# Attention with 32 array rows per head, in units of two heads, on one core

## The reference

```
qkv = layernorm(t) @ w_qkv + b_qkv
attn = softmax((q @ k.T) * HD ** -0.5)
t = t + (attn @ v) @ w_proj + b_proj
```

## Time and profile before

| | |
|---|---|
| median of 3 runs | 281.2 us (280.62 to 281.5) |
| the profiled execution | 279.14 us |
| its span, first to last instruction | 277.3 us |
| mean granted TensorE clock | 0.965 of 2.4 GHz |
| busy | PE 249.7 us (90%), DVE 185.9 (67%), ACT 117.8 (42%), POOL 112.7 (41%) |
| spectral part | 0 to 29.5 us, first tokens and their norm to 36 us |
| attention | 36 to 144 us, first scores at 56.6 us |
| routing, loop, end | 147 to 175, 175 to 258, 258 to 277.3 us |

### The profile page before, as it was taken

How to read it: one execution, slowest core, us unless ns; L and a number is a source line. 1 busy time by engine, 2 the same in 40 slices (tenths; PEclk the granted TensorE clock), 3 DMA queues, 4 the chain that set the end, 5 groups by cost and what they waited for, 6 DMA issues and landing times.

```text
span 277.3 us, 5843 instructions
## 1 busy us (share of the span) xinstructions
PE 249.7 (90%) x2023; PEld 188.2 (68%) x2023; DVE 185.9 (67%) x367; ACT 117.8 (42%) x218; POOL 112.7 (41%) x85
## 2 busy tenths in 40 slices
PE   3999876889999999969888869999999999999982
PEld 3989674777797797658678658455556555554871
DVE  0358699887997998873674883665666666566264
ACT  0370253244153345315523303655765576566303
POOL 8700078672085069100131043265655565653100
PEclk9999995999999999979999798999999999999998
DMA  7989993000000000172388401111111111111163
GB/s 177 248 201 284 273 345 114 0 0 4 2 0 2 0 2 0 53 218 74 111 281 262 143 2 28 28 47 57 43 57 43 53 46 57 42 45 41 40 207 115
DMA packets 24542, 25.97 MB, mean 94 GB/s; under 512 B 5767, under 2 KB 23208, under 8 KB 24520
## 3 DMA queue, kind: packets, MB, share of 16 engines
q1 hardware_dynamic: 20296, 20.30, 24.6%
q0 software_dynamic: 2400, 4.92, 6.0%
q10 hardware_dynamic: 1824, 0.47, 0.7%
HBM read 22.14 MB, written 3.54 MB: 93 GB/s over the span
## 4 chain that ended last, share of the span: by engine, by line
PE 69%; DVE 23%; ACT 2%; issue 2%; DMA 1%; POOL 1%; DVEq 0%
PE bank L1331 10%; PE bank L1359 8%; PE bank L1338 6%; PE bank L1069 5%; PE bank L1222 4%; PE bank L1070 4%; PE bank L1071 4%; DVE main L769 4%; PE bank L1122 4%; PE bank L997 4%; DVE main L758 3%; PE bank L1347 3%; PE bank L1177 3%; DVE main L730 3%; PE bank L1162 2%; PE bank L1045 2%
## 5 line engine op out<-in xcount | busy, mean ns | idle before, releaser
L286 POOL TENSOR_TENSOR rounded<-rounded,cf 128x1536 fp32r<-128x1536 f32 x12 | 38.7, 3243 | 31.0 <-ACT rounded L556 28.3
L1069 PE MATMUL bank<-rounded 128*128 128x256 f32 (+1 forms) x144 | 42.6, 296 | 4.4 <-DVE rounded L764 3.0
L604 ACT ACTIVATE main<-bank 128x512 f32<-128x512 f32 x48 | 28.7, 598 | 37.9 <-PE bank L1071 36.1
L936 DVE COPY main<-main 128x1152 f32 x43 | 33.1, 781 | 16.6 <-issue 14.8
L632 ACT ACTIVATE main<-down_all 128x576 f32 x44 | 30.0, 684 | 28.8 <-PE bank L1359 27.6
L1070 PE MATMUL bank<-rounded 128*128 128x256 f32 (+1 forms) x144 | 41.2, 286 | 0.0
L1071 PE MATMUL bank<-rounded 128*128 128x256 f32 (+1 forms) x144 | 41.1, 286 | 0.0
L758 DVE TENSOR_REDUCE main<-bank 128x2 f32<-128x512 f32 x48 | 31.0, 685 | 7.1 <-PE bank L1122 7.1
L467 POOL DMA_INDIRECT main<-xhat_rows,main x22 | 27.6, 1254 | 19.6 <-PE bank L1319 15.8
L1069 PEld LDWEIGHTS bank<-rounded 128*128 128x128 f32 x144 | 28.2, 196 | 7.7 <-DVE rounded L764 3.5
L475 POOL DMA_INDIRECT pair_rows<-main x20 | 21.7, 1083 | 26.0 <-DVE main L926 26.0
(11 more groups left out here) (164 smaller groups left out, 386.7 us busy)
## 6 DMA issues: line engine op xcount, KB each, us to landing
down_all<-wd SPq DMA_DIRECT2D x16, 288.0 KB, 4.8
main<-wg SPq DMA_DIRECT2D x16, 192.0 KB, 3.2
main<-wu SPq DMA_DIRECT2D x16, 192.0 KB, 2.9
main<-wg SPq DMA_DIRECT2D x16, 96.0 KB, 2.9
main<-wu SPq DMA_DIRECT2D x16, 96.0 KB, 3.3
main<-pair_rows SPq DMA_DIRECT2D x8, 192.0 KB, 3.7
main<-x SPq DMA_DIRECT2D x1, 768.0 KB, 8.0
xhat_rows<-main POOLq DMA_DIRECT2D x8, 96.0 KB, 3.4
```

What stands on the lines that cost most here:

```text
L286: return engine.tensor_tensor(k_sb[part][:, b % 2, t], k_all[part][:, t, :].bitcast(F32).unsqueeze(1).broadcast_to([128, HPT, N]), mask.un ...
L936: vec.tensor_copy(w_gu[:, p, h, :], gu_e(expert(t, h))).then_inc(S["w_gu_ready"], 1)
L1069: mm(dst, w(0), x(0), start=first, stop=False)
```

## The change

- Each head gets 32 array rows of its own: 16 for k times minus one and 16 for k in the columns of `wqkv`, so that against rows of minus the high part of q and of its low part two matmuls of 32 rows make all products, and low by low too. A third, `pick` times `shift`, adds the row of negated maxima. The masked keys are gone, on POOL and on DVE.
- A projection `project_qk(m)` makes a quad of four heads: 12 quads (m = 3 b + g) of 12 matmuls, where it was 4 batches of 24. The matmuls contract 96 or 97 rows, and the memsets of the padding are gone.
- A unit n (24 in all, 6 per batch) is two heads on two neighbouring row groups of 32, with all 256 queries and 256 keys: two banks. `scores_for_max(n)` is 4 matmuls and `scores(n)` 12, in both of which the two heads take turns. The reduction and the exponential take 128x1024 at once.
- `normalise` transposes blocks of 32x32 on DVE, takes the reciprocal of 8 columns, and transposes them back.
- Order: in slot n TensorE takes `scores_for_max(n + 8)` (`LEAD`), then `scores(n)`, then in even slots `project_qk(5 + n // 2)` and `attend(n // 2 - 1)`. Scores have banks 0 and 1, maxima banks 2 and 3 (from unit 16 on the scores use all four in turn), projections bank 4, the output of `attend` bank 6, v and `project_out` bank 7. The two `attend` banks of before become one.
- `w_qkv` comes in 2 DMAs where it was 8, and DVE splits it with 20 instructions where it was 4. 3 experts are loaded at the start, 8 when the tokens are ready, and 5 when all scores are done.

```diff
-HPT = HEADS // 2
+QUAD = 4
+QUADS = HEADS // QUAD
+UNITS = 2 * QUADS
+LEAD = 8
...
-LATE = 12
+MAIN = 37856
+LATE = 5
+BEFORE = 3
...
-        bank = [ctx.enter_context(nc.psum_tensor(f"bank{i}", [128, 512], F32)) for i in range(8)]
+        grid = ctx.enter_context(nc.psum_tensor("grid", [128, QUAD, 512], F32))
+        bank = [grid[:, i, :] for i in range(QUAD)] + [ctx.enter_context(nc.psum_tensor(f"bank{i}", [128, 512], F32)) for i in range(QUAD, 8)]
...
+        def max_banks(n):
+
+            i = 2 if n >= LEAD else 2 * ((n + 1) % 2)
+            return slice(i, i + 2)
+
+        def score_banks(n):
+
+            i = 2 * (n % 2) if n + LEAD >= B * UNITS else 0
+            return slice(i, i + 2)
+
+        def qk_bank(m):
+            return bank[4 + (m % 2 if m < 5 else 0)]
...
+            sp.dma_start(wqkv_raw[0:CH, :, :], a["w_qkv"].rearrange("(k p) n -> p k n", k=2)).then_inc(S["ld_qkv"], 16)
+            sp.dma_start(wqkv_raw[CH:CH + 1, 1, :], a["b_qkv"].unsqueeze(0)).then_inc(S["ld_qkv"], 16)
...
+            sp.wait_ge(S["tok_ready"], B)
+            for e in range(BEFORE, E - LATE):
+                load_expert(e, S["ld_late"])
+            sp.wait_ge(S["st_done"], UNITS * B)
+            for e in range(E - LATE, E):
...
-            for b in range(B):
-                if b >= 2:
...
+            def high_parts(m):
+                b, g = m // QUADS, m % QUADS
+                act.wait_ge(S["qk_done"], m + 1)
...
+                act.activation(qk_hi[:, b % 2, g], qk_bank(m)[:, :].rearrange("p (m n) -> p m n", m=2), ACT.Copy).then_inc(S["qk_high"], 1)
...
+            def shift_rows(b):
+                act.wait_ge(S["rT_done"], b + 1)
+                if b >= 2:
+                    act.wait_ge(S["st_done"], UNITS * (b - 1))
+                act.activation(shift[:, b % 2, :], bank[5][:, 0:N], ACT.Copy).then_inc(S["shift_ready"], 1)
+
+            shift_rows(0)
+            for n in range(B * UNITS):
+                b, u = n // UNITS, n % UNITS
+                quad = n // 2
+                act.wait_ge(S["st_done"], n + 1)
+                if quad >= 2:
+                    act.wait_ge(S["pv_done"], quad - 1)
+                act.activation(probs[:, quad % 2, 2 * (n % 2):2 * (n % 2) + 2, :, :].rearrange("p h k n -> p h (k n)"), grid[:, score_banks(n), :], ACT.Exp).then_inc(S["exp_ready"], 1)
+                if n % 2 == 0 and 5 + n // 2 < B * QUADS:
+                    high_parts(5 + n // 2)
+                if u == 4 and b + 1 < B:
+                    shift_rows(b + 1)
+                if u == 3 and 0 < b < B - 1:
                     values(b + 1)
-                for j in range(3):
...
+            dve.wait_ge(S["ld_qkv"], 2 * 16)
+
+            def columns(x, part, r):
+
+                if part == 2:
+                    return x[0:CH + 1, :, x.shape[2] - C:]
+                if x.shape[2] == 3 * C:
+                    return x[0:CH + 1, :, part * C:part * C + C].rearrange("p k (h d) -> p k h d", d=HD)
+                return x[0:CH + 1, :, part * QK // 2:(part + 1) * QK // 2].rearrange("p k (h r d) -> p k h r d", r=2, d=HD)[:, :, :, r, :]
+
+            for part, r, scale in ((0, 0, SCALE), (0, 1, SCALE), (1, 0, -1.0), (1, 1, 1.0), (2, 0, 1.0)):
+                for k in range(2):
+                    rows = slice(0, CH + k)
+                    vec.tensor_scalar(columns(wqkv[0], part, r)[rows, k], columns(wqkv_raw, part, r)[rows, k], scale, None, ALU.mult).then_inc(S["w_split"], 1)
+            dve.wait_ge(S["w_split"], 10)
+            for part, r, scale in ((0, 0, SCALE), (0, 1, SCALE), (1, 0, -1.0), (1, 1, 1.0), (2, 0, 1.0)):
+                for k in range(2):
+                    rows = slice(0, CH + k)
+                    vec.scalar_tensor_tensor(columns(wqkv[1], part, r)[rows, k], columns(wqkv_raw, part, r)[rows, k], scale,
+                                             columns(wqkv[0], part, r)[rows, k].bitcast(F32), ALU.mult, ALU.subtract).then_inc(S["w_split"], 1)
...
+            def low_parts(m):
+                b, g = m // QUADS, m % QUADS
+                dve.wait_ge(S["qk_high"], m + 1)
+                high = qk_hi[:, b % 2, g].bitcast(F32)
+                vec.scalar_tensor_tensor(q_sb[:, b % 2, g], qk_bank(m)[:, 0:N], low_rows, high[:, 0, :], ALU.mult, ALU.subtract).then_inc(S["qk_split"], 1)
+                vec.tensor_tensor(k_lo[:, b % 2, g], qk_bank(m)[:, N:], high[:, 1, :], ALU.subtract).then_inc(S["qk_split"], 1)
+
+            def maxima(n):
+                b, g, pair = n // UNITS, n % UNITS // 2, n % 2
+                if n == 0:
+                    dve.wait_ge(S["bias_zeroed"], BIAS_SET)
+                dve.wait_ge(S["smax_done"], n + 1)
+                if b >= 2 and n % UNITS == 0:
+                    dve.wait_ge(S["rT_done"], b - 1)
+                col = 64 * pair + g
+                vec.tensor_reduce(negmax[:, b % 2, :, col:col + 33:32].rearrange("p q h -> p h q"),
+                                  grid[:, max_banks(n), :].rearrange("p h (q n) -> p h q n", q=2), AX.X, ALU.max, negate=True).then_inc(S["smax_ready"], 1)
...
             def normalise(quad):
-                b, j, s = quad // 3, quad % 3, quad % 2
+                b, j = quad // QUADS, quad % QUADS
+                pv = bank[6][:, 0:N]
                 dve.wait_ge(S["pv_done"], quad + 1)
-                vec.reciprocal(recip[:, s], bank[6 + s][:, 0:N]).then_inc(S["recip_ready"], 1)
+                vec.transpose(by_query, pv).then_inc(S["by_query_ready"], 1)
+                dve.wait_ge(S["by_query_ready"], quad + 1)
+                vec.reciprocal(recip, by_query[:, HD::32]).then_inc(S["recip_ready"], 1)
                 dve.wait_ge(S["recip_ready"], quad + 1)
-
-                vec.stream_shuffle(den[:, s], recip[:, s], [HD + i % HD for i in range(32)]).then_inc(S["den_ready"], 1)
+                vec.transpose(den, recip.unsqueeze(2).broadcast_to([128, N // 32, 32])).then_inc(S["den_ready"], 1)
                 dve.wait_ge(S["den_ready"], quad + 1)
                 if b >= 2 and j == 0:
                     dve.wait_ge(S["proj_done"], b - 1)
...
-            low_parts(0)
+            vec.tensor_copy(pick, quad_row.unsqueeze(2).broadcast_to([128, QUADS, 128])).then_inc(S["pick_set"], 1)
+            for m in range(QUADS):
+                low_parts(m)
+                if m == 0:
+                    for n in range(2):
+                        maxima(n)
...
-            for b in range(B):
...
+            for n in range(B * UNITS):
+                b, u = n // UNITS, n % UNITS
+                if n + LEAD < B * UNITS:
+                    maxima(n + LEAD)
+                if n % 2 == 0 and n:
+                    normalise(n // 2 - 1)
+                if n % 2 and 5 + n // 2 < B * QUADS:
+                    low_parts(5 + n // 2)
+                if u == 2 and b:
+                    add_attention(b - 1)
+                    if b == B - 1:
+                        statistics(NORM_PARTS[0], "stats2", "mv2", lambda t: dve.wait_ge(S["attn_ready"], t // 2 + 1))
+            normal(NORM_PARTS[0], xhat2, 0, "std2", "rstd2", "xhat2_ready")
             normalise(3 * B - 1)
             add_attention(B - 1)
...
+            def project_qk(m):
+                b, g = m // QUADS, m % QUADS
...
+                elif g == 0:
...
-                    pe.wait_ge(S["w_split"], 4)
-                elif 0 in parts and b == 1:
-                    pe.wait_ge(S["q_low"], 1)
-                elif 0 in parts:
-                    pe.wait_ge(S["smax_ready"], 12 * b)
-                for part in parts:
-                    m, t = 1 - part // 2, part % 2
+
+                if m >= 2:
+                    pe.wait_ge(S["qk_split"], 2 * (m - 1) if m < 6 else 2 * m)
...
-                if part == 3:
-                    last.then_inc(S["qk_done"], 1)
...
+            def scores_for_max(n):
+                b, g, pair = n // UNITS, n % UNITS // 2, n % 2
+                if pair == 0:
+                    pe.wait_ge(S["qk_split"], 2 * (QUADS * b + g) + 2)
+                if n == 0:
+                    pe.wait_ge(S["tok_ready"], B)
+                if n >= 2:
+                    pe.wait_ge(S["smax_ready"], n - 1 if n < LEAD else n)
+                for qh in range(2):
+                    for h in range(2):
+                        rows = slice(64 * pair + 32 * h, 64 * pair + 32 * h + 32)
+                        last = mm(grid[:, max_banks(n).start + h, qh * N:qh * N + N], q_sb[rows, b % 2, g, 128 * qh:128 * qh + 128],
+                                  qk_hi[rows, b % 2, g, 1, :], start=True, stop=True)
+                last.then_inc(S["smax_done"], 1)
 
...
+            def scores(n):
+                b, g, pair = n // UNITS, n % UNITS // 2, n % 2
+                if n % UNITS == 0:
+                    pe.wait_ge(S["shift_ready"], b + 1)
                 if n == 0:
-                    pe.wait_ge(S["xT_low"], B)
-                for v in range(2):
-                    t, h = g6 // 3, (2 * g6 + v) % HPT
```

(59 more changed lines are left out.)

329 lines of the change are left out of this document (105 added, 224 removed).

## The result

The changed kernel takes 301.7 us (median of 4 runs, 299.02 to 307.04) where the kernel before takes 281.35 on the same chip: 1.0635 times as long, 95% interval [1.0562, 1.0708]. Forecast were 274.9 us and a range of 269.5 to 286. The prediction was wrong in sign, and the time lies outside its range. The profiled execution took 299.76 us, its span is 297.8 us, its mean clock 0.857 of 2.4 GHz, where before had 0.965. (The ratio leaves the two longest of the four out; with all four, the medians stand at 1.072.) Executions of the kernel before differ by about 1%, those of the changed one by 2.7%, and the longest has the lowest clock (307.04 at 0.831). I therefore give the range beside each median, and of the variants the clocks as well.

The account below looks back on a forecast made before the run. TensorE was taken to bound attention, DVE close behind. Slot 0 at 61.0, then the cycles, put the last exponential at 129.6 (-5.6); another -0.7 gave 272.8 profiled, plus 2.1 makes 274.9 us, range 269.5 to 286.

Parts of the forecast that it names:

- rival 2: In `scores` and `scores_for_max`, two heads don't overlap; each cycle 0.24 + 0.70 us longer, 286.7 us in all; chance 0.12.
- rival 3: In `normalise`, the transposes cost 0.75 us each; 0.6 more per cycle, 279.8 us in all; chance 0.10.
- The clipping: At the start on DVE, follows the split of `w_qkv`: split from 15.05, 6.2 us long, ending at 21.25.
- Slot 0: End of the prologue: DVE's list of picks, `low_parts`, maxima and waits sums to 61.0 us, where scores started at 56.6.
- The last eight slots: Slots 16 to 23, no maxima and twice the banks: 16.1 us to the end of the last exponential.
- Rival 1: TensorE's 1.95 us gap per cycle lowers the clock: 288.5 us if in all eight cycles, 281.7 in four; chance 0.20.
- the 27 us: Whole profiled execution: forecast 272.8 us, measured 27.0 us longer.
- the 6.15: Slot 0 to the end of the first `attend`: forecast 8.4 us, measured 14.55.
- 2.5 behind it: End of the last exponential to the last `project_out`: forecast 8.2 us, measured 10.7.
- the cycle of 6.6 us: Two slots, one `attend` to the next: 6.6 us, TensorE standing 1.95 of it; five such cycles 33.0 us.
- The projection's own wait: In the two-slot cycle, the projection's wait for the previous quad's `low_parts` ends 0.2 us before it is needed.
- a cycle of 7.4: Attention cycles: any cycle of 7.4 instead of 6.6 us gives all the gain back.

Follow-up runs that it names:

- fillmore: Changed kernel plus matmuls of 96 rows that nobody reads: 14 in odd slots, 16 ahead of slot 0, 20 in the prologue; 287.8 us (278.7 to 295.2).
- hold: leadride32fill with 16 unread matmuls of 128 rows ahead of slot 0 (4 of 96 before) and 14 in odd slots (12 before); 280.9 us (274.9 to 284.3).
- leadfill: Changed kernel with projections one slot pair earlier and unread 96-row matmuls (12 in odd slots, 4 ahead of slot 0, 20 early); 286.9 us (275.1 to 293.9).
- leadride32fill: leadfill with its odd-slot unread matmuls at 128 rows, plus an unread 32-row matmul behind each `scores` pair on an idle row group; 282.9 us (272.5 to 286.9).
- micro: Separate kernel of fp32r matmuls alone, without gaps, in stretches of 128 rows, one, two and four 32-row groups, and 64 rows; 0.1215 us per pair and per four.

## Why the prediction was wrong, point by point

**What held.** The pairs overlap: `scores` 0.71 at full clock, as taken, so rival 2 is out. The reduction of 1024 columns 1.22 us (1.21), the exponential 1.02 (1.05), the transposes 0.45 (0.44), which puts rival 3 out. The clipping follows the weights' split at 20.82 (21.25), but by luck: the load ended near 16.2 and not before 15.05, and the split took 4.6 us, not 6.2. Slot 0 starts at 59.2 (61.0). The last eight slots, without maxima, run at 3.1 to 3.4 us per attend (5.3 with `project_out`).

**Step that failed 1, the clock, which the sum put at nothing in the cycles.** Rival 1, "The gaps cost the clock (0.20)", named the right thing and mis-sized it twice: in chance, and in price. What starts a fall was as it said, a pause near 2 us. Its price, "One fall lasted 3.4 us, which is 1.7 us of work", came from the shorter of the two falls in the kernel before (the other lasted 6.3 us), in stages in which what followed was mostly on 128 rows. Here the clock didn't fall and rise with each gap; behind the pause ahead of slot 0 it went down and stayed for 48 us, 2.97 us per cycle of two slots, through stretches in which TensorE was 100% busy (98.1 to 106.7). The rows that I had taken for it all told of idle time (2.2 us); none had pairs of 32-row tiles in it, since before contracts 128 rows in the scores. That the clock might not come back while half of the array is in use was nowhere in the sum. It took some 22 of the 27 us: 14.1 between the first attend and the last exponential (against fillmore at full clock), about 5 ahead of it (the rest of the 6.15, less one wait of the second step; a remainder, not measured by itself), and most of 2.5 behind it, where the matmuls ahead of `project_out` ran at half clock (154.6 to 160; hold has full clock there, and its 16 matmuls of L1267 take 3.69 us where the changed kernel's of L1244 take 5.37). That the clock is the cause of these is borne out by the executions of leadfill, leadride32fill and hold. Of one program each, the shortest took 275.1, 272.5 and 274.9 us at clocks of 0.962, 0.973 and 0.969; the others took 274.9 to 293.9, at 0.962 and below.

**Step that failed 2, the cycle of 6.6 us.** "The projection's own wait, for `low_parts` of the quad before, is over 0.2 us before it is needed" was said of the projection. `scores_for_max(n + 8)` of the even slot waits for the same `low_parts`, and I had only counted its wait for the maxima. The term "0.04 + normalise 1.6 + maxima 1.21 + 0.05" lacked 0.86 us of `low_parts`: 7.43 measured at full clock, 6.80 where the projections are a pair of slots earlier (forecast 6.6). The prediction said that a cycle of 7.4 gives all back, for eight cycles. The wait comes in six slots, and hold against fillmore puts it at 4.1 us behind the first attend, so with the one ahead of it at about 5: 274.9 would have become about 280, an estimate, where the kernel before takes 281. fillmore's shortest execution, with the wait in it and a clock of 0.977, took 278.7. So this step takes most of the forecast gain but doesn't turn the sign; the clock does.

**The rest of the sum.** Start 1.8 us better than forecast, cycle 0.2 worse than forecast with the wait removed. With both losses gone, the variants run at the forecast in their shortest executions (275.1, 272.5, 274.9), and hold's stretch from the first attend to the last exponential takes 60.5 us (60.2). That is as far as the sum was right. The 1.6 us behind the last `project_out` were not taken apart.

**What stays open.** In the changed kernel the clock falls behind a pause of 2.2 us, in the variants with fillers, near 50 us, behind shorter ones (0.74 and 1.40); the prologue mixes these with 64-row pairs and projections of 96 rows, and no run took them apart. Whether rows in use or the form of the tile keeps it down is argued, not shown. Also open is why executions of one program differ so much here, and only here.

## What to carry to other kernels

Before work is packed onto fewer array rows, price it at both clocks: half the rows for half the time is no gain if the clock halves with it, and a stage of small tiles that starts at 1.2 GHz can stay there even when it is always busy. List for each instruction every semaphore it waits on and what stands ahead of each releaser on its own engine; here the second wait of one instruction was worth about 5 us of a forecast gain of 6.4. And compare executions of one program with their clocks before a variant's median is believed.

## What the runs showed of the hardware that I had not expected

- Busy time alone didn't tell the granted clock. Always busy: one group of 32 rows went from 1.00 to 0.50; pairs of groups stayed at 1.00 if they started there (14.6 us) and at 0.50 if they started there (25.6 us); 96 and 128 rows rose from 0.50 to 1.00. With a pause of 1.85 us in each cycle: 128 rows at 1.00, with 16 pairs between them 0.55. The Trainium skill (TensorE: Matmul & The Clock Gate, HAM oscillation) tells of clocks lost in waits for DMA; the changed kernel lost it behind waits for DVE of 2.1 to 2.2 us, and micro, on one group, without any wait.
- fp32r matmuls of 32 rows, 128 by 256 columns, overlap in full on two groups and on four: 0.1215 us per pair and per four.
- Tiles of 64 and of 32 rows don't overlap: 0.51 us for each change between them at half clock.
- Executions of one program (leadfill) spread by 7% (275.1 to 293.9) on one core, the longer the lower their mean clock; those of the kernel before spread by about 1%.
